# One searched order of steps replaced by another in a four-lane transformer kernel on one core

## What is computed

```
x = x + attention(layernorm(x), ctx)                    # layer A, one head, no projections
x = x + mixed_attention(layernorm(x), 4 experts' Wq, Wk, Wv, top 2 of the gate, Wo)  # layer B, 16 heads
x = x + rope_attention(layernorm(x), ctx, Wq, Wk, Wv, Wo)                            # layer C, 16 heads
x = x + ffn(layernorm(x))                               # layer D:
    # causal attention of 16 heads, y = x + layernorm(attn) * g1 + b1,
    # 8 experts of 128 -> 512 -> 128, top 2 by the gate,
    # y + layernorm(sum of the experts) * g2 + b2
```

## Time and profile before

| | |
|---|---|
| median of 3 runs | 533.73 us (532.73 to 534.79) |
| the profiled execution | 535.21 us, its span 533.4 us |
| mean granted TensorE clock | 0.954 |
| TensorE busy | 471.8 us (88%) |
| TensorE's weight load busy | 385.9 us (72%) |
| ScalarE busy | 371.4 us (70%) |
| VectorE busy | 310.1 us (58%) |
| GpSimd busy | 156.9 us (29%) |
| bytes moved | 10.75 MB |

### The profile page before, as it was taken

How to read it: one execution, slowest core, us unless ns; L and a number is a source line. 1 busy time by engine, 2 the same in 40 slices (tenths; PEclk the granted TensorE clock), 3 DMA queues, 4 the chain that set the end, 5 groups by cost and what they waited for, 6 DMA issues and landing times.

```text
span 533.4 us, 18187 instructions
## 1 busy us (share of the span) xinstructions
PE 471.8 (88%) x7456; PEld 385.9 (72%) x7456; DVE 310.1 (58%) x940; ACT 371.4 (70%) x914; POOL 156.9 (29%) x397
## 2 busy tenths in 40 slices
PE   4576777777799999999999999999999999999894
PEld 3344545554578787888887877887778878889793
DVE  3368578558436658775576868575753737232211
ACT  4566655776757787888888878878777785665452
POOL 5425121320241214454462213201331441242302
PEclk9995978999759999999999999999999999999998
DMA  7900000000000000000000000000000000000000
GB/s 238 370 21 17 1 1 3 3 1 4 2 1 2 3 4 1 14 3 1 2 12 2 2 2 14 2 2 3 3 13 2 1 12 3 2 11 1 11 2 10
DMA packets 6776, 10.75 MB, mean 20 GB/s; under 512 B 464, under 2 KB 6056, under 8 KB 6312
## 3 DMA queue, kind: packets, MB, share of 16 engines
q1 hardware_dynamic: 6696, 9.60, 5.2%
HBM read 8.55 MB, written 1.05 MB: 18 GB/s over the span
## 4 chain that ended last, share of the span: by engine, by line
PE 70%; DVE 11%; ACT 7%; issue 4%; POOL 4%; DMA 3%; SPq 1%; POOLq 0%; DVEq 0%; ACTq 0%
PE bk L611 20%; PE bk L601 8%; PE bk L659 5%; DVE negmax L1003 5%; PE bk L660 5%; PE bk L661 5%; PE bk L587 3%; ACT w1f L778 3%; DMA w1f<-in_w 3%; PE bk L580 2%; PE bk L557 2%; PE bk L458 2%; PE bk L520 2%; PE bk L573 2%; PE bk L506 2%
## 5 line engine op out<-in xcount | busy, mean ns | idle before, releaser
L611 PE MATMUL bk<-w2f,hT 128*128 128x128 f32 x1024 | 135.6, 276 | 1.8 <-ACT hT L804 1.8
L804 ACT ACTIVATE hT<-bk,pk 128x256 f32<-128x256 f32 x256 | 107.1, 476 | 37.9 <-PE bk L661 37.3
L611 PEld LDWEIGHTS bk<-w2f,hT 128*128 128x128 f32 x1024 | 124.4, 192 | 4.7 <-ACT hT L804 2.0
L778 ACT ACTIVATE w1f<-bk 128x512 f32<-128x512 f32 (+1 forms) x192 | 98.5, 602 | 26.1 <-PE bk L587 25.7
L1003 DVE TENSOR_REDUCE negmax<-bk 128x4 f32<-128x512 f32 (+1 forms) x192 | 104.9, 611 | 16.3 <-PE bk L587 15.7
L934 DVE SCALAR_TENSOR_TENSOR acc<-bk,comb,acc 128x128 f32<-128x128 f32 x128 | 38.8, 345 | 71.9 <-PE bk L611 71.6
L659 PE MATMUL bk<-yhi,w1hi 128*128 128x256 f16 x256 | 70.7, 276 | 0.0
L661 PE MATMUL bk<-yhi,w1lo 128*128 128x256 f16 x256 | 70.4, 275 | 0.0
L660 PE MATMUL bk<-ylo,w1hi 128*128 128x256 f16 x256 | 70.4, 275 | 0.0
L1036 POOL TENSOR_SCALAR shift<-mv 128x2 f32<-128x2 f32 x40 | 10.0, 251 | 190.0 <-DVE mv L944 189.2
L601 PE MATMUL bk<-w1f,val 128*32 128x128 f32 (+1 forms) x1536 | 55.5, 290 | 1.3 <-ACT w1f L778 1.2
(11 more groups left out here) (152 smaller groups left out, 780.3 us busy)
## 6 DMA issues: line engine op xcount, KB each, us to landing
w1f<-in_w SPq DMA_DIRECT2D x1, 2048.0 KB, 14.8
w2f<-in_w SPq DMA_DIRECT2D x1, 2048.0 KB
pk<-in_pack SPq DMA_DIRECT2D x1, 1690.0 KB, 7.8
xin<-in_x SPq DMA_DIRECT2D x8, 128.0 KB, 2.4
out<-outb SPq DMA_DIRECT2D x8, 128.0 KB, 1.8
cin<-in_ctx SPq DMA_DIRECT2D x8, 77.0 KB
hf<-in_half SPq DMA_DIRECT2D x1, 416.0 KB, 10.4
rw<-in_rows SPq DMA_DIRECT2D x1, 320.0 KB, 8.4
```

What stands on the lines that cost most here:

```text
L611: last = mm(o[:, i * D:(i + 1) * D], hT[:, k % HRING, i * T:(i + 1) * T], w2f[:, k, :], start=c == 0 and i == 0, stop=c == CH - 1, skip_gr ...
L778: act.activation(probs[0:nk, ring(n, q), :], bank(g, st, q)[0:nk, :], ACT.Exp, scale=SCALE[L]).then_inc(s_exp, 1)
L804: act.activation(hT[:, k % HRING, :], bank(g, st)[:, m * W:(m + 1) * W], ACT.Relu, bias=P("b1")[:, k:k + 1]).then_inc(s_relu, 1)
```

## The change

Both strings are replaced; nothing else is touched. The new ones come from a search with a model in which TensorE's clock is cold in the first stretch. Each step has the same instructions as before. Two lines of each table:

```diff
 ORDER = (
-    "0100212001033011011020150202130512032155503012303300220532505321003213100321012020002022023003200223"
+    "2002011330102101023012311203012032502055153130521032052100003551000321202032201321020203200131230020"
...
 TAKEN = (
-    "0123456701234560712345607123450672134506721304536721045672310456731045627310456273140562731264705312"
+    "0123456701234567012345670123456071234560723415605723410657234106573541063754210635746216035127460351"
```

More of the change, by code:

```diff
@@ L106 @@
 ORDER = (
[L107 to L113, removed]
+    "2002011330102101023012311203012032502055153130521032052100003551000321202032201321020203200131230020"
+    "1202103100231230203121030123023100230210131020302102021302303023132031021310031002003102321031032101"
+    "2300441402201412314104103314231021421034010141204021342130431014201213410411403212140102341304241142"
+    "4404424134102342001243021410114301420122430142031240124012331241312444142343214023441204321314032100"
+    "4313424333021432312042130431031412344412301303414431202034013220040312142330143201040132041224013024"
+    "4021033210033102124100324130402311403410323420431012342344341243243142314324311423213414232131142341"
+    "4221343243234433214342144334434422434423244243242244424442432444434343444334434434344444444344444444"
     "444444444444"
@@ L118 @@
 TAKEN = (
-    "0123456701234560712345607123450672134506721304536721045672310456731045627310456273140562731264705312"
[L120 to L128, removed]
+    "0123456701234567012345670123456071234560723415605723410657234106573541063754210635746216035127460351"
+    "2704635172046317204361720436172043567120546307512467350162735062730564127530642753076425317046253014"
+    "7623501647123502645710326457103247510247150243715023471560234715602436710526431065324106752413064752"
+    "1063452106375120463725160347516034207531460746530127463501742601743260157463250174353017645031724652"
+    "4036157425036412703645127035415270631456273456271453602751630274516027453106274510271435072164530712"
+    "6430674123567041267054132670513267561320756320754613207563421075304752136407523160735214067521740562"
+    "3741056237401256724015724031574263507142630271436027531467054631751463075124360725136407256134057263"
+    "4052063412506137250163472041632705413257041362570643254701325740136275410362534160275341602715463027"
+    "1463025463072543172564017325164703517642703651240735124601735426703154726305472605341263057416207451"
+    "260754126407512360745213067524106372540163725410673245160723"
 )
```

## The result

| | before | after |
|---|---|---|
| median | 533.36 us (532.73 to 534.79) | 543.27 us (540.51 to 543.75) |
| profiled execution, its span | 535.21, 533.4 us | 543.75, 541.9 us |
| mean granted TensorE clock | 0.954 | 0.964 |
| TensorE busy | 471.8 us | 477.9 us |

The account below looks back on a forecast made before the run. Taken as decided in the first 161 us, where lanes' chains through in-order engines, not work, mostly bind; TensorE binds afterwards. Opening -2.4 and wait -1.0, other terms 0, sum to -3.4: 533.7 to 530.3 us, range 521.5 to 540.5.

Parts of the forecast that it names:

- The opening, -2.4 us: Start through lane 0's first exponentials and PV: -1.5 and -0.9 us, ends -5 and +3.
- the same time as before: Lane 0's eight reductions, at 40.27 us before, were to start unchanged because steps ahead of them were already done.
- What I had taken out behind them: After lane 0's reductions, lane 3's transpose and lane 2's logits leave the cold stretch: -1.3 us, exponentials at about 47.1.
- the loss at the mix: Lane 0's B.mix, at 27.54 us before, expected at about 30.5 us: +3.0.
- the other end, +3: Upper end for the opening: +3 us if lane 0's loss at the mix is never won back.
- my three signs of being wrong: First L580 after 49.5 us; experts' first matmul later than 157 us at equal work; idle past 165 us above 8 us.
- 51 to 136 us, 0: Equal work in another weave of the lanes: 0, with -4 and +4 us as ends.
- The wait at 138 us, -1.0: TensorE's 2.09 us wait for lane 3's normalised rows gets covered by other steps: middle of -2.1 and 0.
- The clock, 0: Clock likeliest falls again somewhere between 100 us and the first expert pieces, so no gain: 0.
- My slower rival: Clock falls earlier, from about 118 us, and stays low until the experts: +9.2 us, 539.5 us; chance 0.20.
- The rival in which the stretch disappears: Cold stretch before the experts vanishes: -5.8 and -2.6 us, together -8.4, so 521.9 us; chance 0.18.
- 161 us to the end, 0: TensorE-bound expert stretch, 6.3 us idle in 329: 0, with -1 and +2 us as ends.

Follow-up runs that it names:

- fill-ins: Extra matmuls on a tile of ones in TensorE's waits: old order 523.15 us (37 places), new order 532.36 us (37) and 529.83 us (45).
- Plain banks: Either order with each use taking the PSUM bank that came free first, instead of the search's bank table: old 539.08 us, new 543.99 us.

## Why the prediction was wrong

**The opening, -2.4 us: the step that failed first.** Its early part held. TensorE's first instruction started at 6.77 us (6.6 predicted), lane 0's first transpose at 8.99 (8.7), B.mix at 30.02 (30.5). Then I followed lane 0 alone through the steps that had left its way, and didn't ask what had come into it. The operand of lane 0's stacking was ready at 38.13 us, but the new order has lane 2's B.lg ahead of it, and that waited 2.35 us (from 36.2 to 38.59 us) for ScalarE's L723, which stood behind lane 3's norm: the stacking started at 39.53 us, 1.4 us after it could, where I had 37.8. (Lane 1's B.hid, with its wait of 3.07 us, stands ahead of lane 0's mix, but the mix then waited 0.45 us more for its own operand, so that wait cost lane 0 nothing.) I had also put the eight reductions at "the same time as before" though the stacking ahead of them was 1.1 us late by my own sum; they began at 42.98 us, 2.7 later. What I had taken out behind them held nearly: with the clock up, 7.1 us from the first reduction to the first exponentials' matmul against 8.1, -1.0 for -1.3. So the first exponentials came not at 47.1 but at 50.78 us in the profile; with the clock up at 34 us, as in the run with the opening alone, at 49.65 (reductions at 42.54). I had put the loss at the mix at +3.0 and had most of it won back by this; it wasn't, which I had named as the other end, +3. Measured alone the opening costs 1.5 us (clock as it falls) or 2.4 us (fill-ins, 1.3 of it by the fall at 50.7 us). Of my three signs of being wrong two came: the first L580 after 49.5 us, the experts' first matmul at 160.11, past 157.

**51 to 136 us, 0.** At 60 us of work after was 3.8 us behind, with 1.3 us less idle time than before (37.6 against 38.9): it had 5.1 us more of busy time, by the low level that held to 56 us. With the clock kept up it was 2.5 us behind (118.8 against 116.3), near the opening's own price. So 0 for the weave isn't refuted, but no run here isolates it, and the distance jumps by more than 1 us around that point.

**The wait at 138 us, -1.0.** I counted the work that covers lane 3's late norm. It does cover it. But the covering steps wait for their own exponentials and evictions on ScalarE: in all six waits, 4.2 us, for one of 2.09. Between 60 and 90 us of work TensorE idles 8.0 us against 6.0; in the steps 180 to 200 it is 3.8 against 2.4. A gap that is filled with steps of other lanes is filled only if these are ready. With the clock high in both profiles the stretch from 60 to 90 us of work takes 44.0 against 42.4 us, +1.6; the distance jumps there too, and with the points moved by a us of work it comes out at 3 to 4 us. So the sign is read from the two profiles; the size is somewhere from 1.6 to 4 us, and no run isolates it.

**The clock, 0.** Over the medians it was small but not nothing: with the clock kept up, the distance of 9.9 us shrinks to 6.7, so some 3 us of it are the clock's. (The fill-ins stand in other places in the two orders, and the new one's clock still fell in some executions, so this isn't a clean separation.) My slower rival had the mechanism in part: in the profile the low level did cost the change more, but by a start that stayed low until 56 us and by the same 20.5 us around the experts at the old length, not by an earlier fall. Even that is one execution's: the new order with the old end had 48 and 13.7 us, the old order with the new end 52 and 13.7. That the measured time lies above the rival's 539.5 us doesn't confirm it. The forecast that a fall stays was right. (The rival in which the stretch disappears had a slip: with nine tenths at the low level, 16.7 us of busy time are 9.2 us at the high level, not 8.7, which makes its -5.8 some -5.1 us and its time 522.6 for 521.9.)

**161 us to the end, 0, with +2 as the end.** It cost 2.0 us from step 584 on (128.1 against 130.0 us), wherever it was put. I had looked at the last turnover and at the total idle time of the old order, 6.3 us, and had read it as what an order could win; it says nothing of what another order can lose. This was the surest of the losses and the one that one comparison of the two lists at a step where both have done the same could have shown: ahead of step 584 the volume is equal, and what follows has lane 3's norm 0.93 us and one more operand 0.64 us too late.

**In sum.** Of the 9.9 us, by the medians, the clock has 3.2 (9.9 - 6.7), the end 2.0, and what stands ahead of step 584 with the clock kept up the other 4.7. Of these 4.7 the opening has 1.1 to 2.4; the rest, 2.3 to 3.6, lies behind it, by the profiles mostly between 60 and 90 us of work, at the entry to the experts. The failed terms are so -2.4 (measured +1.1 to +2.4), -1.0 (+1.6 or more) and 0 (+2.0). The shares ahead of step 584 are read from profiles and in part argued. The term for the clock can't be had closer: executions of the kernel before lay between 529.7 and 537.1 us, and the scatter is at least in part that of the clock's rises and falls.

**The rule.** The Trainium skill (TensorE: Matmul & The Clock Gate, "What's actually happening") says that the cold count varies from run to run and is not to be fitted. The runs agree on that: the low level at the start lasted until 29 to 31 us in five profiles with the old opening and until 52 us in a sixth, and with the new opening until 33 to 34 us in four, 48 in one and 56 in the change's own. On its size, under 1% of a typical span, they don't contradict it: keeping the clock up gives the old order 10.5 of 533.7 us, 2.0%, but that is the start and four later falls together. A model in which the first stretch is cold plans for a start that isn't fixed, as these lengths show.

## What to carry to other kernels

- When a step leaves the critical chain, look at what entered it, on every engine that issues in order: a step of another lane ahead of it makes its own wait everybody's wait. Check a gap's cover for whether each covering step is itself ready.
- Compare two orders at a point where both have done the same set of steps, and cut there in experiments too. Count the matmuls on both sides of the comparison: if they differ, the windows don't hold the same steps. Such a cut gave 128.1 us for the old end behind either order, while cuts elsewhere added some 2 us of waits of their own.
- Take no cause from one profile of each when the clock rises and falls: the same 584 steps took 411.9 us in one profile and 406.2 in another.
- Where TensorE waits often in a stretch, matmuls that nobody reads, placed in the waits, were worth 10.5 us to the old order (2.0%), and its five runs lay within 1.4 us; the other order that the search gave lost 9.9.

## What the runs showed of the hardware

- The granted clock rises and falls at different places in executions of the same instructions: with the same first 584 steps the first rise was at 31 and at 52 us (old order), at 56 and at 48 us (new order). L498 (eight matmuls) took 1.14 us at 34.0 us in the run with the new opening alone and 2.06 us in after, with the same first 69 steps.
- The profile's clock column reads 1.00 until its first change, whatever the level is. The duration of a known record shows the level: L481 of four 1.22 or 1.06 us against 0.61.
- The clock fell at 148.4 us behind a row of waits of 0.71 to 1.04 us, where before it fell behind one of 2.09. It stayed down for 20.5 us in both, though TensorE was busy for all of the last 8.8 us of it in after. In the two profiles with the ends exchanged it stayed down there for 13.7 us.
- Plain banks at the same order cost the old order 6.0 us and the new 0.7. Which waits make it was not read from the traces; in the old order's profile 2.6 us of it are a fall of the clock at 501 us.
